# The router's products in pairs, and three small moves at the start and the end of a mixture-of-experts kernel

## The reference

```python
# layer 0: a product whose input is scaled per batch, output rescaled per batch
ys = y / sqrt(512)
d = rsqrt(einsum('bi,io->bo', ys*ys, W*W) + 1e-8)
x1 = x + einsum('bsi,io->bso', x * ys[:, None, :], W) * d[:, None, :]
# layer 1: a shared expert and 8 routed ones, the best 2 of each token
shared = silu(x1 @ w1) * (x1 @ w3) @ w2
s = sigmoid(concat([x1, t_emb]) @ router_W)          # 8 values a token
# top 2 of s + router_bias, their s normalised to gates
routed = sum over the 2 chosen experts of gate * (gelu(x1 @ W1e[e]) @ W2e[e])
out = x1 + (shared + routed) / 3
```

## Time and profile before

| | us |
|---|---|
| median of 3 runs | 1030.64 |
| lowest, highest | 1030.07, 1032.32 |
| the profiled execution | 1030.44 |
| its span | 1028.6 |
| stage 1, from the first real matmul | 7.0 to 104.7 |
| stage 2 | 106.3 to some 635 |
| stage 3, to the last matmul | to 1020.4 |

### The profile page before, as it was taken

One profiled execution on the slowest core, in us unless ns is written; L12 is line 12 of the kernel. 1 busy time (PEld: TensorE's weight loads), 2 busy tenths in 40 slices (PEclk: granted clock), 3 DMA queues, 4 the chain that ended last, 5 costly groups with the idle time before them and its releaser, 6 DMA issues.

```text
span 1028.6 us, 15045 instructions
## 1 busy us (share of the span) xinstructions
PE 1015.4 (99%) x4686; PEld 836.0 (81%) x4686; DVE 518.8 (50%) x846; ACT 292.6 (28%) x461; POOL 317.2 (31%) x389
## 2 busy tenths in 40 slices
PE   8999999999999999999999999999999999999996
PEld 6888788888888888888888888788888888888885
DVE  7555546567334434334322215656665656666653
ACT  4233432222223222222221113333333333332331
POOL 0000000002232333324322402365554554554543
PEclk9999999999999999999999999999999999999998
DMA  5766555635878898888963586899999999999975
GB/s 181 259 225 225 204 187 185 231 111 179 306 248 279 266 313 307 278 317 254 324 236 113 195 204 200 209 213 232 225 189 223 213 223 226 208 228 227 214 150 84
DMA packets 133267, 228.70 MB, mean 222 GB/s; under 512 B 29041, under 2 KB 83953, under 8 KB 125105
## 3 DMA queue, kind: packets, MB, share of 16 engines
q1 hardware_dynamic: 61264, 145.10, 43.7%
q0 software_dynamic: 31328, 64.11, 27.1%
q10 hardware_dynamic: 40608, 18.64, 8.0%
HBM read 112.85 MB, written 98.38 MB: 205 GB/s over the span
## 4 chain that ended last, share of the span: by engine, by line
PE 88%; DMA 4%; issue 3%; POOLq 2%; POOL 2%; DVE 0%; ACT 0%; ACTq 0%
PE banks L499 11%; PE banks L500 11%; PE banks L501 11%; PE banks L568 9%; PE banks L569 9%; PE banks L570 9%; PE banks L513 6%; PE banks L515 6%; PE banks L514 6%; DMA out<-ys,slot 4%; PE banks L436 3%; PE banks L437 2%; PE banks L438 2%; POOLq L1233 2%; POOL out L1242 1%
## 5 line engine op out<-in xcount | busy, mean ns | idle before, releaser
L499 PE MATMUL banks<-xh,w 128*128 128x512 f32 x512 | 199.6, 390 | 0.6 <-DVE xl L767 0.6
L500 PE MATMUL banks<-xl,w 128*128 128x512 f32 x512 | 199.2, 389 | 0.0
L501 PE MATMUL banks<-xh,w 128*128 128x512 f32 x512 | 199.2, 389 | 0.0
L1242 POOL DMA_INDIRECT out<-ys,slot x71 | 116.5, 1641 | 187.1 <-DVE ys L1136 87.9
L840 DVE SCALAR_TENSOR_TENSOR gm<-sil,banks 128x512 f32<-128x512 f32 x64 | 44.0, 687 | 254.5 <-ACT sil L654 254.4
L654 ACT ACTIVATE sil<-banks 128x512 f32<-128x512 f32 x64 | 38.3, 598 | 343.6 <-PE banks L501 343.6
L1226 POOL DMA_DIRECT2D xg<-xs_d x136 | 100.6, 1138 | 48.0 <-DVE xgt L1097 48.0
L499 PEld LDWEIGHTS banks<-xh,w 128*128 128x128 f32 x512 | 96.1, 188 | 20.9 <-issue 1.1
L568 PE MATMUL banks<-we,xgth 128*128 x284 | 110.9, 390 | 1.7 <-issue 1.7
L501 PEld LDWEIGHTS banks<-xh,w 128*128 128x128 f32 x512 | 96.1, 188 | 20.0
L500 PEld LDWEIGHTS banks<-xl,w 128*128 128x128 f32 x512 | 96.1, 188 | 19.8
(11 more groups left out here) (177 smaller groups left out, 1449.5 us busy)
## 6 DMA issues: line engine op xcount, KB each, us to landing
we_d<-ehl SPq DMA_DIRECT2D x32, 1024.0 KB, 6.7
we<-we_d SPq DMA_DIRECT2D x48, 512.0 KB, 6.0
hturn<-hid ACTq DMA_DIRECT2D x280, 64.0 KB
xg<-xs_d POOLq DMA_DIRECT2D x136, 128.0 KB, 6.5
eraw<-expert_w SPq DMA_DIRECT2D x32, 512.0 KB, 5.3
x1t_d<-x1t SPq DMA_DIRECT2D x8, 1024.0 KB, 9.2
xin<-x1t_d SPq DMA_DIRECT2D x8, 1024.0 KB, 9.1
x_d<-x1tok SPq DMA_DIRECT2D x32, 256.0 KB, 4.9
```

The source lines that it names most:

```text
L499: pe.matmul(ps[hc % 2][:, :], w_hi, xh[:, j, c, :], start=(c == 0), stop=False)
L500: pe.matmul(ps[hc % 2][:, :], w_hi, xl[:, j, c, :], start=False, stop=False)
L501: last = pe.matmul(ps[hc % 2][:, :], w_lo, xh[:, j, c, :], start=False, stop=(c == DC - 1))
L1242: pool.indirect_dma_start(out[:, :], IO(slot[:, t, 0:1], 0), ys[:, t % RING, :], None, compute_op=ALU.add).then_inc(added[t % RING], 16)
```

## The change

- PE: nine matmuls on zeros instead of ten. `logits` no longer stands behind each `linear`. Behind `linear(2)`, `linear(4)` and `linear(6)` stand those of two blocks (0 and 1, 2 and 3, 4 and 5), behind `linear(7)` those of block 6, and behind `linear(1)`, `linear(3)` and `linear(5)` none.
- DVE: in blocks 2, 4 and 6 the four low parts of the next block come ahead of the four evictions. In block 7 the low parts of chunks 0, 1 and (2, 3) follow the evictions of o = 0, 1 and 2. In blocks 1, 3 and 5 the order stays.
- ACT issues the first chunk of x first. The load of `cnd` goes to POOL.
- POOL: `read_waits(t + 1)` reads the table values of the next tile ahead of the waits of tile t.

```diff
             pe.wait_ge(zeros_done, 1)
-            for _ in range(10):
+            for _ in range(9):
                 pe.matmul(lin_ps[4][:, :], zeros[:, 0:P], zeros[:, :], start=True, stop=True)
...
             for n in range(1, NBLK):
                 linear(n, n % 2)
                 if n == 1:
                     condition_logits()
-                logits(n - 1, (n - 1) % 2)
+                for m in ((n - 2, n - 1) if n % 2 == 0 else (n - 1,) if n == NBLK - 1 else ()):
+                    logits(m, m % 2)
...
-            act.dma_start(cnd[:, :, :], condT).then_inc(cond_in, 16)
             act.dma_start(xin[:, 0, 0, :], xT[0, :, 0, :]).then_inc(x0_in[0], 16)
...
             for n in range(NBLK):
                 j = n % 2
+                early = 0 < n < NBLK - 1 and n % 2 == 0
+                for c in range(DC if early else 0):
+                    scaled_low(n + 1, c)
                 for o in range(DC):
...
-                    for c in (() if n == 0 else (o,) if n == NBLK - 1 else ((), (), (0,), (1, 2, 3))[o]):
+                    for c in (() if n == 0 or early else ((0,), (1,), (2, 3), ())[o] if n == NBLK - 1 else ((), (), (0,), (1, 2, 3))[o]):
                         if n + 1 < NBLK:
                             scaled_low(n + 1, c)
...
         def _(pool):
             IO = bass.IndirectOffsetOnAxis
+            pool.dma_start(cnd[:, :, :], condT).then_inc(cond_in, 16)
...
+            landed = [{} for _ in range(TILES + 1)]
+
+            def read_waits(t):
+
+                if t < TILES:
+                    for b in range(1, RING):
+                        if t - b >= RING:
+                            landed[t][b] = pool.value_load(wait_for[0:1, b - 1, t:t + 1], min_val=16, max_val=16 * (TILES // RING + 2))
+
             def scatter(t):
...
-                landed = {b: pool.value_load(wait_for[0:1, b - 1, t:t + 1], min_val=16, max_val=16 * (TILES // RING + 2))
-                          for b in range(1, RING) if t - b >= RING}
                 for b in range(1, min(t, RING - 1) + 1):
...
-                        pool.wait_ge(added[(t - b) % RING], landed[b])
+                        pool.wait_ge(added[(t - b) % RING], landed[t][b])
...
-                if t == RING + 1:
+                if t == RING:
                     pool.wait_ge(waits_done, RING - 1)
+                read_waits(t + 1)
                 scatter(t)
```

## The result

The changed kernel takes 1035.09 us (median of 7 runs, 1033.7 to 1037.0), the kernel before 1030.92 beside it (7 runs, 1030.07 to 1032.32). The ratio is 1.0038, 95% interval 1.0026 to 1.0049: slower by some 4 us. I had forecast 1032.3 and a range to 1034.0. The profiled execution took 1036.34 us, its span 1034.5, so it is itself 1.25 above the median; what is known of that spread stands at the end of the part on the prediction.

The account below looks back on a forecast made before the run. PE bounds the kernel, busy 1015.4 of 1028.6 us. Terms -0.40 -0.15 +0.81 +0.05 +0.81 +0.05 +1.55 -1.0 sum to +1.7 us, on 1030.64 giving 1032.3; range of 8 in 10: 1030.7 to 1034.0.

Parts of the forecast that it names:

- I take nothing for this: At the start, cnd issued by POOL at about 0.85 and landing at 3.7 was to cost nothing.
- the -0.40 for x's chunk: At the start, issuing x's first chunk earlier on ACT was to gain 0.40 us, with ends at -0.44 and nothing.
- this as a rival with 0.12: At the start, cnd by POOL lands at 7.4, first matmul at 8.4: total +3.5, 1034.1 us; chance 0.12.
- The chunk's 0.44: At the start, x's first chunk is issued at 0.85, 0.44 us earlier, gaining 0.44 if its load lasts as long.
- The steps on the pairs: Stage 1 boundaries: two groups cost +0.81 us each at 2 to 3 and 4 to 5; no group +0.05 each at 3 to 4, 5 to 6.
- The bare boundaries: Boundaries 3 to 4 and 5 to 6, without router products: PE waits for DVE's low part as long as was saved, +0.05 us each.
- A pair's second group: Second group of router products directly behind another on PE: 0.81 us, at most 1.01.
- Chunk 2 behind a bare boundary: Boundaries without router products: chunk 2 starts at T + 2.48 against T + 2.43 before; T ends a linear's last matmul.
- boundary 1 to 2: Between blocks 1 and 2, the condition's products hide part of the wait: chunk 2 at 34.28 against 34.43, -0.15 us.
- The way into stage 2: From block 6 to stage 2, xin lands later and delays DVE's low parts: +1.55 us, including the third pair's 0.81.
- the end: Last two scatters: reading table values ahead moves the last one forward, -1.0 us, with ends -0.7 and -1.1.
- the longer way from there to the end: At the last scatter, its landing beside the previous scatter's ends last, so nothing is gained: +2.7, 1033.3 us; chance 0.10.

Follow-up runs that it names:

- the start alone: Kernel before with cnd loaded by POOL, x's first chunk first on ACT and nine matmuls on zeros: 1033.56 us, ratio 1.0017.
- the run with the old start: Changed kernel with the start as before (cnd first on ACT, then x, ten zeros): 1034.72 us, ratio 1.0026.
- the run with both loads on ACT: Kernel before with ACT's two loads exchanged, x's first chunk first and cnd second, ten zeros: 1033.07 us, ratio 1.0013.
- the two-pair version: Kernel before with router pairs only behind linear(2) and linear(4), low parts ahead in blocks 1 and 3, block 7's low parts moved, table values read ahead: 1029.91 us.
- the low parts ahead: Kernel before with the change's pairs and DVE order, plus all four low parts ahead of the last eviction in blocks 1, 3, 5: 1032.71 us, ratio 1.001.
- the fourteen zeros: Kernel before with cnd on POOL, x's first chunk first on ACT and 14 matmuls on zeros: 1032.46 us, ratio 1.0009.
- the read-ahead alone: Kernel before with only the table values read ahead: 1030.69 us, ratio 0.9997.
- two pairs with twelve zeros: The two-pair version with twelve matmuls on zeros instead of ten: 1030.08 us, ratio 0.9985 of the kernel before.
- block 7 alone: Kernel before with only block 7's low parts of chunks 2 and 3 moved behind the eviction of o = 2: 1030.98 us, ratio 1.0001.

## Why the prediction was wrong

The step that failed is "I take nothing for this", on `cnd` behind POOL, and with it the -0.40 for x's chunk. Together they were to be -0.40; the trace has +3.87, and the start alone costs 1.9 in the medians. With the -0.40 that is 2.3 of a miss of 2.5 (+4.2 against +1.7), though the run with the old start gives the start less, as said there. Three things were wrong in it.

- *The price of the small load.* I took 2.8 us from a load that ran when little else did and argued that the queues are empty at its issue. It took 5.58, from an issue 0.47 later than I had it. The bound from the other side, 6.5, was near. That the DMA engines had nothing to do at its issue did not help: its packets moved between 3.7 and 6.4, among those of the loads beside it, and on ACT behind the chunk it lands near 6.2 as well. I had this as a rival with 0.12, and the rival came true, with the first matmul at 8.15 where it had 8.4. Its sum, 1034.1, lay just above the end of my range.
- *The chunk's 0.44.* I moved one transfer and left the others where they were. The chunk and the first weights exchange their landings, and the weights are followed by two steps on ACT. This alone puts the first matmul 0.5 late, in the run with both loads on ACT.
- *The pace of PE's first matmuls.* The forecast and the rival both took them at 0.23 us. From the first real matmul to L428 it takes 24.05 us before, 25.67 in the start alone and 26.74 in the profiled execution of the changed kernel, that is, 1.6 and 2.7 more. In the start alone the clock fell behind a gap of 2.06 us. In the changed kernel's profile it had not risen yet, and the gap is not shown to be why: x's chunk first (gap 0.88, 1.7 more) and the two-pair version (gap 0.52, 1.9 more) have the same, while the low parts ahead (gap 1.21) and the fourteen zeros (gap 0.87) lose nothing. How often this happens with each start is open, so this part of the loss, unlike the late first matmul, may be luck of the execution in part.

The steps on the pairs held. The bare boundaries stall as described, and the run with the low parts ahead shows the cause. Their size was too high: from L428 to block 6's end I had +1.57, the trace has +0.93. A pair's second group costs 0.88 (47.28 to 49.17 is 1.89, less 1.01) against 0.81. Chunk 2 behind a bare boundary starts at T + 2.29 (62.65 - 60.36) instead of T + 2.48: I took 0.26 from DVE to PE from one place, where PE waits for several things, and it is 0.04 here (61.80 to 61.84). At boundary 1 to 2 it is T + 2.59 (37.64 - 35.05) instead of T + 3.10: `xin` landed 0.3 sooner, so low part 0 held up the eviction by 0.3 less, and DVE to PE is 0.04 here too.

The way into stage 2 was right in mechanism and size: SP issues at 101.32, T + 4.0 (3.9 forecast), PE starts at T + 15.26 (15.3), +1.5 (1.55). On the end I forecast the last scatter 1.7 to 1.9 behind the one before and it is 1.85; the longer way from there to the end, which I had as a rival, takes half of the gain back. Had the start been as before, my sum would have stood at +2.1 for pairs and read-ahead; the ratio of the run with the old start gives +2.7 with an interval of +0.9 to +4.4.

Open: in every kernel here, before too, some executions lie 1.5 to 3 us above the lowest, a few up to 10. Part of it can be when TensorE steps up: in the profiles of the changed kernel, x's chunk first and the two-pair version it is at 11 to 14 us, in that of before by the end of the zeros, and 1.7 to 2.7 us hang on it. Another part can be the standing time at L568 in stage 3, 1.5 to 4.4 us over these profiles. I have no run that fixes either.

## What to carry to other kernels

A piece of work that stands between two stages of the bounding engine may be the cover of another engine's chain: before it is moved or merged, follow that engine's order up to what the bounding engine needs next, and move that chain first. In the start measured here, advancing one load delayed another. So cost the whole order of landings and not one transfer, and give a small load that everything waits for the first place. Price a wait of TensorE of 2 us or so with the matmuls behind it, and do not take the first microseconds of a kernel at the full pace.

## What the runs showed of the hardware

- Gaps of PE of 0.6 to 1.6 us, once TensorE had stepped up (the longest 1.56 ahead of stage 2 with the old start, 1.62 in stage 3 of the read-ahead alone) left the granted clock at 1.00. It was 0.50 for 3.4 us behind gaps of 1.86 us (two pairs with twelve zeros, stage 3), 2.06 us (new start alone), 2.50 us (low parts ahead) and 2.85 us (block 7 alone, stage 3). At this level the matmuls were 0.43 us apart, and then 0.23 again. In the second case the level fell only 1.0 us after PE had begun again.
- At the start TensorE steps up at a time that differs between executions: with much the same zeros from 1.94 on, the spacing became 0.23 at 5 to 6 us in eight profiles, at 7 to 8 in three (ten, twelve and fourteen zeros), at 11 in two, and near 13.9 in that of the changed kernel.
- The clock column is 1.00 from 0 on even where the matmuls on zeros run 0.43 apart, until the first change that is on record. At the start only the spacing of the matmuls tells the level.
- An 8 KB load issued behind a 256 KB one landed near 6.2 us on ACT's queue and at 6.8 to 7.5 by POOL, and at 3.1 to 3.5 when it was issued first.
- Two indirect scatters started 1.85 instead of 2.78 us apart: from the start of the second to the end took 0.5 us longer (mean of five profiles against nine).
